# Three routed expert layers: one stage each, a table made by TensorE, rows gathered per expert tile

## What is computed

```python
# L1_ffn (called m1): the best two of 8 experts for each token
h = _layernorm(x, ln2_g, ln2_b).reshape(B * S, D)
logits = h @ gate_w + gate_b
topv, topi = jax.lax.top_k(logits, TOPK)
gw = jax.nn.softmax(topv, axis=-1)
ew = jnp.sum(jax.nn.one_hot(topi, E, dtype=h.dtype) * gw[..., None], axis=1)
hid = jax.nn.relu(jnp.einsum('td,edf->etf', h, W1) + b1[:, None, :])
out_e = jnp.einsum('etf,efd->etd', hid, W2) + b2[:, None, :]
moe = jnp.einsum('etd,te->td', out_e, ew)

# L2_ffn (m2): every expert whose sigmoid gate is over 0.5
probs = jax.nn.sigmoid(x_flat @ Wg + bg)
mask = (probs > THRESHOLD).astype(x_flat.dtype)
weights = probs * mask      # then relu experts with b1, b2 as above

# L3_ffn (m3): the best expert, gelu, no biases
route = jax.nn.sigmoid(x @ Wr + br)
max_prob = jnp.max(route, axis=1, keepdims=True)
max_ind = jnp.argmax(route, axis=1)
```

## Time and profile before

| | |
|---|---|
| median of 3 runs | 2763.42 us (2761.18 to 2769.22) |
| the profiled execution | 2774.48 us, its span 2772.7 us |
| TensorE busy | 2119.2 us (76% of the span), mean granted clock 0.875 |
| VectorE, ScalarE, POOL busy | 1248.5, 828.2, 443.2 us |
| DMA, mean over the span | 57 GB/s |

### The profile page before, as it was taken

How to read it: one execution, slowest core, us unless ns; L and a number is a source line. 1 busy time by engine, 2 the same in 40 slices (tenths; PEclk the granted TensorE clock), 3 DMA queues, 4 the chain that set the end, 5 groups by cost and what they waited for, 6 DMA issues and landing times. The chain is left out here.

```text
span 2772.7 us, 39418 instructions
## 1 busy us (share of the span) xinstructions
PE 2119.2 (76%) x11925; PEld 1548.1 (56%) x11929; DVE 1248.5 (45%) x2841; ACT 828.2 (30%) x1718; POOL 443.2 (16%) x363
## 2 busy tenths in 40 slices
PE   6689979368899898255999634899998981993398
PEld 5477746122222222144999533788888871683297
DVE  6856621868777773342333343222222222673221
ACT  2404421113555556001333210233333330341021
POOL 0100000010000000033222103334524530000322
PEclk9899989677999999557999865999999996995699
DMA  3012110130101100712222253222222212007111
GB/s 129 1 43 74 46 33 4 37 102 13 36 24 32 28 25 7 244 50 75 33 33 33 53 194 107 54 43 48 58 39 47 48 31 57 1 1 274 55 30 27
DMA packets 128820, 157.19 MB, mean 57 GB/s; under 512 B 24266, under 2 KB 108499, under 8 KB 128693
## 3 DMA queue, kind: packets, MB, share of 16 engines
q1 hardware_dynamic: 100661, 123.14, 14.3%
q0 software_dynamic: 28032, 32.60, 6.7%
HBM read 110.32 MB, written 57.24 MB: 60 GB/s over the span
## 5 line engine op out<-in xcount | busy, mean ns | idle before, releaser
L1454 PE MATMUL banks<-m_rowsT,x_normT 128*128 128x128 f32 x4032 | 487.0, 280 | 46.1 <-DVE m_rowsT L1516 22.9
L1454 PEld LDWEIGHTS banks<-m_rowsT,x_normT 128*128 128x128 f32 x4032 | 473.3, 195 | 76.8 <-issue 65.2
L1464 PE MATMUL banks<-e_w,m_hT 128*128 x2016 | 456.7, 379 | 3.6 <-ACT m_y L1549 2.6
L1464 PEld LDWEIGHTS banks<-e_w,m_hT 128*128 128x128 f32 x2016 | 373.1, 190 | 50.8 <-issue 5.4
L1539 ACT ACTIVATE m_hT<-banks,m_bias 128x128 f32<-128x128 f32 x848 | 241.1, 370 | 402.5 <-PE banks L1454 384.5
L1839 DVE TENSOR_REDUCE sh_mhalf<-banks 128x1 f32<-128x512 f32 x512 | 318.9, 684 | 76.1 <-PE banks L1742 71.4
L1817 ACT ACTIVATE sh_pT<-banks 128x1024 f32<-128x1024 f32 x256 | 249.5, 1021 | 210.5 <-PE banks L1795 210.5
L1411 POOL DMA_INDIRECT scratch_acc<-m_y,m_ids x106 | 175.8, 1659 | 538.0 <-ACT m_y L1549 487.2
L1520 DVE COPY m_ids<-m_rows 128x1 int32<-128x1 int32 x126 | 19.4, 154 | 509.7 <-POOLq L1417 410.5
L1742 PE MATMUL banks<-sh_ks,sh_qs 96*128 96x512 bf16 x512 | 196.1, 416 | 53.8 <-DVE sh_mhalf L1839 33.4
L1501 DVE TENSOR_SCALAR x_normT<-e_w 128x2048 f32 x129 | 159.7, 1238 | 137.6 <-PEq L1470 81.9
(11 more groups left out here) (317 smaller groups left out, 2485.5 us busy)
## 6 DMA issues: line engine op xcount, KB each, us to landing
e_w<-L_W SPq DMA_DIRECT2D x32, 1024.0 KB, 12.2
m_rows<-scratch_rows SPq DMA_DIRECT2D x126, 132.5 KB, 2.1
e_w<-L1f_W SPq DMA_DIRECT2D x16, 1024.0 KB, 12.1
a_bt<-bias SPq DMA_DIRECT2D x16, 616.0 KB, 4.1
scratch_parts<-sp_part SPq DMA_DIRECT2D x48, 128.0 KB, 1.9
sh_qs<-scratch_parts SPq DMA_DIRECT2D x96, 64.0 KB, 2.6
sh_ks<-scratch_parts SPq DMA_DIRECT2D x96, 64.0 KB, 2.7
scratch_acc<-x_resid SPq DMA_DIRECT2D x2, 2048.0 KB
```

What stands on the lines that cost most here:

```text
L1454: mm = pe.matmul(ps[:, H_BANK + f // 4, f % 4 * P:(f % 4 + 1) * P], w1_tile[:, u, k, f * P:(f + 1) * P], rowsT[:, u, k, :], start=(k == 0) ...
L1464: mm = pe.matmul(ps[:, Y_BANK, 0:D], hT[:, u, f, :], w2_sb[:, bass.ds(e, 1), f, :], start=(f == 0), stop=(f == FB - 1))
```

## The change

- `Routing`, `Gate`, `route`, `load_experts` and `routed_feed_forward` go; `routed_layer` is one stage with norm, gate, routing and experts. The expert weights are loaded by SP inside it, small parameters, the row table and x are moved on ACT's queue.
- The residual add of m1 moves from VectorE to POOL.
- Ranks: the running sums over tiles are built in PSUM by 17 bf16 matmuls instead of 16 dependent VectorE adds.
- No rows are sent to slots. The normalised rows and their weights are stored once, in token order (`table`, with one zero row at index 2048). VectorE makes one-hot masks of each choice's lane and tile (bf16), and TensorE multiplies them into `ids`: for each expert tile and lane the number of its token. Slots without a token get 2048.
- In the loop POOL copies the tile's column of `ids`, gathers 128 rows by an indirect read two tiles ahead, and scatters the results. It waits for a scatter before the next one instead of behind it. Row, output, weight and id buffers are four (`RING`) instead of two; the loop body holds two pairs.
- The PSUM banks of transposes, first and second product are double. ScalarE handles activation and scaling of the same tile in one step, and TensorE's order of products stays as it was.
- VectorE no longer copies token numbers per tile.

The core of the diff (`first`, `second` and the masks' arithmetic left out where nothing is said of them):

```diff
-            def load(s, u):
-                for k, start in enumerate(starts):
-                    with sp.If(start == s):
-                        sp.wait_ge(routing.rows_out[k + 1], 16 * NT)
-                sp.wait_ge(rT_mm, s + 1)
-                sp.wait_ge(tail_in, s + 1)
-                sp.dma_start(rows[:, u, :], dram["scratch_rows"].rearrange("(s p) d -> p s d", p=P)[:, bass.ds(s, 1), :]
-                             .rearrange("p s d -> p (s d)")).then_inc(rows_in[u], 16)
...
+            for e in range(EXPERTS):
+                sp.dma_start(w1_sb[:, e, :, :], w1[e].rearrange("(k p) f -> p k f", p=P)).then_inc(experts_in, 16)
+                sp.dma_start(w2_sb[:, e, :, :], w2[e].rearrange("(f p) d -> p f d", p=P)).then_inc(experts_in, 16)
...
-            def add_rows(s, u, i):
+            if joined:
+                pool.tensor_tensor(x[:], x[:], src[:], ALU.add).then_inc(added, 1)
...
+            def gather(s, v):
+                if local:
+                    at = pool.value_load(column[0:1, bass.ds(s, 1)], min_val=0, max_val=COLS + 1)
+                else:
+                    at = s
+                pool.tensor_copy(row_ids[:, v:v + 1], ids[:, bass.ds(at, 1)]).then_inc(ids_in, 1)
+                pool.wait_ge(ids_in, s + 1)
+                pool.sem_inc(ids_seen, 1)
+                pool.indirect_dma_start(rows[:, v, :], None, table, bass.IndirectOffsetOnAxis(ap=row_ids[:, v:v + 1], axis=0),
+                                        bounds_check=TOK, oob_is_err=False).then_inc(rows_in[v], 16)
+
+            def add_rows(s, u, v, i, last_pair):
+                with pool.If(i < last_pair):
+                    gather(s + 2, (v + 2) % RING)
                 pool.wait_ge(y_sb, s + 3)
-                pool.sem_inc(y_taken, 1)
-
-                pool.indirect_dma_start(stream, bass.IndirectOffsetOnAxis(ap=ids[:, u:u + 1], axis=0), y[:, u, :], None,
-                                        bounds_check=TOK - 1, oob_is_err=False, compute_op=ALU.add).then_inc(y_out, 16)
-                if routing.by_expert:
-                    send_rows(i, u)
                 pool.wait_ge(y_out, s * 16 + 16)
                 pool.sem_inc(y_free, 1)
+                pool.indirect_dma_start(stream, bass.IndirectOffsetOnAxis(ap=row_ids[:, v:v + 1], axis=0), y[:, v, :], None,
+                                        bounds_check=TOK - 1, oob_is_err=False, compute_op=ALU.add).then_inc(y_out, 16)
+
+            pool.wait_ge(ids_done, 1)
+            pool.wait_ge(stored, 16 * 3)
+            for s in range(2):
...
+            pool.wait_ge(x_stored, 16)
+            last_pair = each_tile(pool, add_rows)
...
+            def transpose_rows(s, u, v):
+                pe.wait_ge(rows_in[v], (s - v) * 4 + 16)
                 pe.wait_ge(rT_sb, s + 1)
                 for k in range(KD):
+                    mm = pe.transpose(ps[:, R_BANK[u], k * P:(k + 1) * P], rows[:, v, k * P:(k + 1) * P], core.ident[:])
                 mm.then_inc(rT_mm, 1)
...
                     for s, u in ((i * 2 + 1, 1), (i * 2 + 2, 0)):
                         first(s, u)
-                        transpose_rows(s + 1, 1 - u)
+                        transpose_rows(s + 1, 1 - u, (2 * h + 3 - u) % RING)
                         second(s - 1, 1 - u)
...
+            link(dve.tensor_tensor(tile_hits, tiles_b[:].unsqueeze(1).unsqueeze(1).broadcast_to([P, G, NT, W]),
+                                   tile_at[:].unsqueeze(3).broadcast_to([P, G, NT, W]), ALU.is_equal))
...
+            for g in range(G):
+                if g >= 2:
+                    dve.wait_ge(table_mm, g - 1)
+                dve.tensor_tensor(lane_hits[:, g % 2], lanes_b[:].unsqueeze(1).broadcast_to([P, NT, P]),
+                                  lane_at[:, g, :].unsqueeze(2).broadcast_to([P, NT, P]), ALU.is_equal).then_inc(lanes_done, 1)
```

More of the change, by code:

```diff
@@ L976, in _ @@
                                          ALU.mult, ALU.add).then_inc(y_sb, 1)
[L979 to L1011, removed]
@@ L1014 @@
[L1014 to L1035, removed]
@@ L1360, in each_pair @@
             if group == S // 2:
-                with eng.Fori(0, group) as i:
-                    step(i)
+                with eng.Fori(0, group // 2) as i:
+                    for h in range(2):
+                        step(i * 2 + h, h)
             else:
@@ new lines, in _ @@
+            pool.memset(pad_row[:], 0.0).then_inc(pad_ready, 1)
+            pool.memset(ones_b[:], 1.0).then_inc(made, 1)
+            pool.memset(chosen[:, NT, :], 0.0).then_inc(made, 1)
+            pool.memset(pad_id[:], float(TOK)).then_inc(made, 1)
+            pool.wait_ge(made, 3)
+            pool.tensor_copy(ids[:, COLS:COLS + 2], pad_id[:].broadcast_to([P, 2])).then_inc(made, 1)
+            pool.wait_ge(params_in, PARAMS)
+            pool.tensor_copy(before_b[:], before[:]).then_inc(made, 1)
@@ new lines, in _ @@
+            for t in range(NT):
+                if t % 4 == 0:
+                    pe.wait_ge(evac_act, t // 4 + 1)
+                    pe.wait_ge(evac_dve, t // 4 + 1)
+                for k in range(KD):
+                    mm = pe.matmul(ps[:, 0, t * EXPERTS:(t + 1) * EXPERTS], xnT[:, k, t * P:(t + 1) * P], wg_sb[:, k, :],
+                                   start=(k == 0), stop=(k == KD - 1))
+            mm.then_inc(g_mm, 1)
+            pe.wait_ge(made, 8)
+            pe.wait_ge(chosen_done, 1)
@@ new lines, in _ @@
+            act.activation(std[:], moments[:, :, 1], ACT.Sqrt).then_inc(std_done, 1)
+            act.wait_ge(params_in, PARAMS)
+            for g in range(NCH):
+                act.wait_ge(transposed, 2 * g + 1)
+                to, from_ = xnT[:, 0, g * CH:(g + 1) * CH], ps[:, 2 * g, :]
+                if affine is not None:
+                    act.activation(to, from_, ACT.Identity, bias=s_sb[:, 0:1], scale=g_sb[:, 0:1]).then_inc(evac_act, 1)
+                else:
+                    act.copy(to, from_).then_inc(evac_act, 1)
```

621 lines of the change are left out of this document (315 added, 306 removed).

## The result

The changed kernel takes 3284.5 us (median of 4 runs, 3279.0 to 3287.4), the kernel before 2763.5 (4 runs, 2761.2 to 2769.2): a ratio of 1.188, 95% interval 1.185 to 1.190, so 521 us slower. The forecast was 3174, with a range of 2850 to 3320. The profiled execution has a span of 3277.2 us, 504.5 more than before, at a mean granted clock of 0.857.

The account below looks back on a forecast made before the run. The prediction took the old expert loop as TensorE-bound and m1's head as bound by issue and POOL. A new gather chain would cost 628 us, heads and m2's end give 217: +411, 3174 us, range 2850 to 3320.

Parts of the forecast that it names:

- Heads and m2's end: Routed layers' starts and the wait after m2's last scatter: gains of 192 and 25 us, together 217.
- Length of the chain: Expert loop, second product's end through output, scatter, id copy and gather to the next transposes: 7.3 us per tile.
- Transposes to second product: Expert loop, TensorE's stretch from row transposes to second product: 0.22 us per tile.
- 117: Loop periods in which the chain closes, 35 + 17 + 65, all but each layer's first two and last tile.
- The clock: Expert loop: TensorE idle time lowers its clock, adding 2.0 us per tile (1.3 to 2.6), for a 13.1 us period.
- rival A: Expert loop: the clock holds at full despite idle time, period 11.15 us, total 2945 us; chance 28%.
- Sum: Whole kernel: loops lose 628 us, heads and m2's end gain 217, net +411, giving 3174 us.
- Rivals B and C: Expert loop: first, shorter chain, period 10.2, 2835 us, 8%; second, quicker scatter and gather, 2722 us, 5%.
- L: Expert loop: time from the second product's end to the transposes of gathered rows, put at 7.3 us.
- break-even in L (5.75): Expert loop: chain length at which loop loss eats the 217 us gain, 5.75 us; below it the change wins.
- break-even in the period (9.6): Expert loop: time per tile at which loop loss eats the 217 us gain, 9.6 us.
- signs to look for: Profile after: DMA wait at transposes in almost every tile, outputs near 13 us apart, gather 4.3 us after second product.

Follow-up runs that it names:

- the idle products: Changed kernel plus 26 or 13 useless identity matmuls on TensorE before its wait for gathered rows: 3224.2 us with 26, 3105.1 us with 13.
- the gather ahead of the scatter: Changed kernel with the gather of tile s + 3 issued after the wait for tile s's output but before its scatter: 2987.4 us, ratio 1.077.
- L = 4.6: Changed kernel with the gather issued before the scatter and its ids copied a tile earlier: 2793.1 us, ratio 1.011.
- the ids early: Changed kernel with the next gather's ids copied before POOL waits for the output, gather still behind the scatter: 3240.2 us, ratio 1.172.
- the early register read: Changed kernel with TensorE reading the expert's number before its wait for the gathered rows: 3217.4 us, ratio 1.160.
- as is: The changed kernel without further edits, against the kernel before: 3284.5 us, ratio 1.188.
- one link more: Changed kernel with a second copy of the ids and a second wait between scatter and gather: 3335.1 us, ratio 1.207.

## Why the prediction was right, and where it was off

The direction, the mechanism and its place were right, and the miss is of size: undone alone, the two-tile distance gives back 761 us (3284.5 to 2523.1).

- *Heads and m2's end, 217 forecast, 206 measured.* The cancelling parts: in m1 from stage start to gate 29.7 us (1125.45 to 1155.15 in the trace) where 18 stood in the sum. I had charged the move of the addition to POOL 1.7 us, by its duration only. It starts 10.7 us into the stage, then the norm and the pad row (and so ScalarE's square root) wait for it. The gate matmuls took 11.1 (12.4), the top-2 chain 4.2 (4.2), ranks and links 5.3 (5.7), masks 8.0 (8.5), and b2 13.8 beyond the ids (9). In m2 the eight lane masks took 17.7 (17.6). In m3 the weights decided, as said, but in 60.8 us, not 52. I left out the 2 MB store of x to the output, with which the head moves 21 MB, at 376 to 399 GB/s over most of it; held back, it gave 4.7 of these 8.8 us.
- *Length of the chain, 7.3 forecast, 7.17 measured.* Handing over (1.06 for 1.3) and gather (2.95 for 3.0, in bounds of 2.4 to 3.6) held. The copy of the ids was misread in both directions: it takes 0.76 us, not 0.1, but 0.55 of that lies beside the end of the scatter, and the wait behind it 0.85. The estimate of 2.3 us for the gather, worked out from the Trainium skill's page "DMA: Bandwidth & Descriptors" (section "Anatomy of one DMA — SWDGE (gpsimd) path"), was too short against the 2.95 of the trace.
- *Transposes to second product, 0.22 forecast, 1.05 measured.* This term failed. The earlier trace rows have 0.22 with a queue that ran ahead; the register read with a standing queue was not in my list. 0.83 × 117 = 97 us, as much as the whole miss of 94 between the profiled executions; the smaller errors nearly cancel. (Between the medians the miss is 110: the forecast was put on a median 11 below its profiled execution, and the profiled one after is 5 below its median.) Taking the read out gave 67 us, not 97, so this is arithmetic of one tile and not the read's price.
- *The clock, 2.0 forecast, 1.75 measured,* within its bounds of 1.3 to 2.6, and shown by the idle products. Its nearness is partly luck: in most tiles the second product took whatever filled the spacing up to 13.6 us, 5.2 to 6.2 us for chains within 0.75 us of this one, so a chain shorter by 0.7 us than the one forecast would have moved the time by only 44 to 67 us. The bare chain is 11.9 rather than 11.15, so rival A, a clock that holds, would have given not 2945 but about 3069 (3284.5 − 1.75 × 123).
- *Sum.* The period was 13.65 for 13.1, which is 64 us in 117; the loops took 711 for 628, so 19 more lie in the tiles at their ends that the 117 left out, and were not taken apart; the heads make the other 11.
- *Rivals B and C* needed a shorter chain. With the gather ahead of the scatter L is 5.1 in m1 and 5.7 in m2 (7.17 less 2.1 and 1.5), on both sides of C's 5.4 with its period of 9.24 and 2722 us. It has 9.7 at its shortest, 10.4 in the mean of m1 and 11.7 of m2, and 2987 us; even L = 4.6 is 1.1% slower than the kernel before. So my break-even in L (5.75) was wrong, for want of the 0.8 us behind the transposes and of any clock loss at short idle times, while the break-even in the period (9.6) held to 1.1% of the kernel's time.
- *Of the signs to look for,* the DMA wait at the transposes stood in 117 of 126 tiles, all in which the chain can close, the spacing was 13.7 (13 said), the gather started 4.2 us after the second product's end (4.3 said).

Open: why POOL's addition of m1 starts 10 to 14 us into the stage in every kernel that has it there; no run here separates its causes. The only other addition of that shape on POOL, 96 to 100 us into every kernel, starts behind 6.9 to 7.1 us for which nothing in the profile stands either. How the clock decides in which tiles of an even loop it falls was not tried.

## What to carry to other kernels

When a load moves into the in-order stream of an engine that also waits for results, follow the chain from result to next load: if it closes within the loop, its length and not the engines' work is the period, and one more buffer of distance can be worth all of it. Idle time on TensorE cost more than its length here, and shortening the chain by less than took it out of the idle range gave back only half of what was taken off (44 of 91 us). A move to an idle engine is priced by when that engine starts and who waits, not by the instruction's duration.

## What the runs showed of the hardware

- The price of a microsecond of chain was not even: by the medians and 123 tiles each microsecond cost 1.1 us upward (for 0.37), gave 0.5 and 0.85 downward (for 0.74 and 0.65), and 1.4 for 1.74 in the mean. The mean granted clock was lower in the kernels with the somewhat shorter chain (0.821 with the ids early, 0.829 with the early register read) than as is (0.857) or with one link more (0.847).
- With chains from 0.74 us shorter to 0.37 longer, 48 to 92 of 123 spacings stayed at 13.4 to 13.8 us, and the second product took 5.2 to 6.2 us in them. Behind an idle time of 2.8 us it ran at 0.57 in one tile and at 1.00 in another.
- On POOL an indirect DMA starts 0.85 us after POOL's own copy that it waits for, and 0.98 after ScalarE's output (1344.40 to 1345.38); a copy that waits for a copy starts after 0.17, one that waits for ScalarE's output after 0.4. Without a wait one indirect DMA follows another after 0.31.
- A 128x1 copy on POOL took 0.76 us when it began beside the end of a scatter's issue, and 0.18 to 0.20 alone.
- A register read in TensorE's queue cost 0.65 us behind a wait (1.07 to 0.42 us from transposes to second product); where TensorE's queue ran ahead that stretch was 0.22 with the read in it.
